# Attention and mixture of experts: one payload row for both experts, four payload and output buffers, neighbouring result rows

## What is computed

```python
h = layer_norm(x, ln1_w, ln1_b)
wei = softmax(where(causal, q @ k.T * C**-0.5, NEG_INF))   # 4 heads of 32, within a batch of 32 tokens
x = x + (wei @ v) @ Wo + bo
nx = layer_norm(x, ln2_w, ln2_b)
noisy = nx @ Wr + br + noise * softplus(nx @ Wn + bn)       # 8 experts
router_out = softmax(noisy with all but the top 2 at NEG_INF)
non_skip = sigmoid(nx @ Wsk + bsk) <= 0.5
expert_out = sum over e: router_out[e] * (relu(nx @ W1[e] + b1[e]) @ W2[e] + b2[e])
final = where(non_skip, x + expert_out, x)
```

## Time and profile before

| what | value |
|---|---|
| median of 3 executions | 811.3 us (807.3 to 813.56) |
| the profiled execution, its own time | 814.46 us |
| its span, first to last instruction | 812.5 us |
| busy share of the span | PE 71%, PEld 56%, DVE 71%, ACT 60%, POOL 51% |
| mean granted TensorE clock | 0.865 of 2.4 GHz |
| packets of the DMA queues | 164172, 127.32 MB |
| "instruction" packets in queues q8 and q14 | 27 and 17 |

### The profile page before, as it was taken

How to read it: one execution, slowest core, us unless ns; L and a number is a source line. 1 busy time by engine, 2 the same in 40 slices (tenths; PEclk the granted TensorE clock), 3 DMA queues, 4 the chain that set the end, 5 groups by cost and what they waited for, 6 DMA issues and landing times.

```text
span 812.5 us, 31537 instructions
## 1 busy us (share of the span) xinstructions
PE 579.6 (71%) x11012; PEld 455.5 (56%) x11012; DVE 576.5 (71%) x2270; ACT 486.9 (60%) x979; POOL 413.0 (51%) x478
## 2 busy tenths in 40 slices
PE   0466989989998998998865209999999999700000
PEld 0245767767776776777645207777777777500000
DVE  3366767887878788787664626777777777537887
ACT  2447666877877788687654208888888888400000
POOL 3000656677766777666655741666666666430000
PEclk9989989999999999999976559999999999855555
DMA  9764222332332332235443257777776777159997
GB/s 95 233 193 122 62 84 76 96 101 59 98 96 59 98 98 85 75 100 112 121 142 96 97 186 258 235 230 235 234 237 235 238 234 238 49 143 292 301 301 223
DMA packets 164172, 127.32 MB, mean 157 GB/s; under 512 B 38050, under 2 KB 142595, under 8 KB 164128
## 3 DMA queue, kind: packets, MB, share of 16 engines
q1 hardware_dynamic: 127264, 90.00, 37.8%
q10 hardware_dynamic: 24576, 20.98, 8.6%
q0 software_dynamic: 12288, 15.77, 6.1%
HBM read 73.86 MB, written 62.78 MB: 168 GB/s over the span
## 4 chain that ended last, share of the span: by engine, by line
PE 41%; DVE 22%; issue 14%; DMA 7%; ACT 5%; POOL 4%; DVEq 3%; ACTq 2%; SPq 1%; POOLq 0%
PE ps L547 6%; PE ps L504 6%; DMA out<-z 5%; DVE stats L830 4%; PE ps L569 4%; POOL expert_rows L1135 3%; PE ps L637 3%; PE ps L585 3%; PE ps L638 3%; PE ps L639 3%; PE ps L625 3%; PE ps L627 3%; PE ps L626 3%; DVE sc_m L873 2%; DVE smax L870 2%
## 5 line engine op out<-in xcount | busy, mean ns | idle before, releaser
L1135 POOL DMA_INDIRECT expert_rows<-pay,rows_of x256 | 254.2, 993 | 195.0 <-DVE rows_of L929 116.1
L1147 POOL DMA_INDIRECT expert_results<-z,words x128 | 135.1, 1055 | 106.9 <-DVE z L1028 75.6
L675 ACT ACTIVATE z<-xres,shift,rstd 128x128 f32 (+1 forms) x256 | 105.1, 483 | 34.4 <-DVE shift L864 34.4
L1042 DVE TENSOR_TENSOR hlo<-h,hhi 128x512 fp32r<-128x512 f32 x128 | 89.7, 701 | 45.7 <-ACT hhi L788 43.6
L786 ACT ACTIVATE h<-ps,w1x 128x512 f32<-128x512 f32 x128 | 88.3, 690 | 34.8 <-PE ps L627 31.3
L788 ACT ACTIVATE hhi<-ps,w1x 128x512 fp32r<-128x512 f32 x128 | 87.3, 682 | 0.0
L547 PEld LDWEIGHTS ps<-pT,v_sb 32*32 32x32 f32 x4096 | 48.4, 106 | 66.0 <-issue 64.6
L547 PE MATMUL ps<-pT,v_sb 32*32 32x32 f32 x4096 | 58.0, 204 | 35.7 <-DVE sc_m L873 25.2
L504 PE MATMUL ps<-ident,z 128*128 128x128 f32 x256 | 46.3, 310 | 25.8 <-ACT z L675 20.0
L637 PE MATMUL ps<-hhi,w2x 128*128 128x512 f32 x128 | 57.3, 447 | 4.2 <-issue 4.2
L527 PE MATMUL ps<-kT,qT 32*32 32x32 f32 x4096 | 55.8, 201 | 3.9
(11 more groups left out here) (147 smaller groups left out, 1321.5 us busy)
## 6 DMA issues: line engine op xcount, KB each, us to landing
w1x<-split_weights SPq DMA_DIRECT2D x33, 514.0 KB, 3.7
w2x<-split_weights SPq DMA_DIRECT2D x33, 512.5 KB
expert_results<-zeros SPq DMA_DIRECT2D x32, 512.0 KB
pay<-expert_rows SPq DMA_DIRECT2D x33, 264.0 KB, 3.6
xres<-in_r_x SPq DMA_DIRECT2D x32, 256.0 KB
split_weights<-w2x ACTq DMA_DIRECT2D x16, 512.0 KB
hhi<-expert_results SPq DMA_DIRECT2D x32, 256.0 KB, 3.7
hlo<-expert_results SPq DMA_DIRECT2D x32, 256.0 KB, 3.8
```

The lines of the kernel that those rows point to most:

```text
L675: m = nc.scalar.activation(z[:, j:j + 1], tile(xres, n, j), ACT.Identity, bias=shift[:, which, j:j + 1], scale=rstd[:, which, j:j + 1])
L1042: ev.tensor_tensor(hlo[:, c], h32[:, c % 2], hhi[:, c].bitcast(F32), ALU.subtract).then_inc(s_h_lo, 1)
L1135: g.indirect_dma_start(rows, bass.IndirectOffsetOnAxis(ap=rows_of[:, odd, k * J + j:k * J + j + 1], axis=0), pay[:, odd, k, j, :], None, b ...
L1147: g.indirect_dma_start(results, bass.IndirectOffsetOnAxis(ap=words[:, slot, j:j + 1], axis=0), yrow[slot][:, j, :], None, bounds_check=K * ...
```

## The change

- The payload is one row for both experts, with four buffers: `pay` is [P, 4, J, RW], as large as before. The second norm writes its rows into it in place, and TensorE transposes them from there. The copy L754 and its semaphore go.
- Word 128 is 2 x token. It is copied by ScalarE from a constant `words_all` just before the second norm. Words 129 and 130 are the token's two expert numbers (0 where the token skips), written by VectorE where it wrote `top_f` before. Pool's two operations a group go.
- `keep_words` makes the result's row from the row: word 128, plus 1 if word 129 is not this block's expert number (`exp_no`, one more operation for the table).
- `results` has a token's two results next to each other, so one DMA a group loads both, 1 KB a token.
- The combining accumulates in place in one of four `fin` buffers, and waits for the store of four groups before, ahead of its first half.
- `pipeline` has a body of four steps for all engines, since the payload's buffer number must be a constant in the code.

The diff, cut to its core:

```diff
-    results_t = results.rearrange("(k n p) c -> p k n c", k=K, p=P)
+    results_t = results.rearrange("(n p k) c -> p n k c", k=K, p=P)
...
-        pay = sb("pay", [P, 2, K, J, RW])
+        words_all = sb("words_all", [P, N // P])
+        pay = sb("pay", [P, 4, J, RW])
...
-        half = z1
-        fin = z2
+        fin = [z1[:, 0], z1[:, 1], z2[:, 0], z2[:, 1]]
+
+        xg = [pay[:, i] for i in range(4)]
...
         def pipeline(eng, step):
 
             for t in range(-2, 5):
-                step(t, t % 2)
-            with eng.Fori(5, NG - 4, 2) as t:
-                step(t, 1)
-                step(t + 1, 0)
+                step(t, t % 4)
+            with eng.Fori(5, NG - 6, 4) as t:
+                for d in range(4):
+                    step(t + d, (5 + d) % 4)
             for t in range(NG - 3, NG + 3):
-                step(t, t % 2)
+                step(t, t % 4)
...
-                for k in range(K):
-                    sp.dma_start(yin[slot][:, k], results_t[:, k, bass.ds(n * J, J), :]).then_inc(f_in[slot], 16)
+                sp.dma_start(yin[slot], results_t[:, bass.ds(n * J, J), :, :]).then_inc(f_in[slot], 16)
...
-                    transposes(ps[:, 6, :], z2[:, par], s_z2T_made)
+                    transposes(ps[:, 6, :], pay[:, (turn + 2) % 4, :, 0:C], s_z2T_made)
...
                     act.wait_ge(s_norm, (t + 3) * NORM)
-                    wait(act, s_z2T_made, n - 1)
-                    norm_rows(z2[:, par], 1, n).then_inc(s_z2, 1)
+                    slot = (turn + 2) % 4
+                    wait(act, sent[slot], quad(n, slot, SENT))
+                    nc.scalar.activation(pay[:, slot, :, C], words_all[:, bass.ds(n * J, J)], ACT.Copy)
+                    norm_rows(pay[:, slot, :, 0:C], 1, n).then_inc(s_z2, 1)
...
-                    wait(act, sent[par], pair(n, par, SENT))
-                    nc.scalar.activation(pay[:, par, :, :, 0:C], z2[:, par].unsqueeze(1).to_broadcast([P, K, J, C]),
-                                         ACT.Copy).then_inc(s_pay_made, 1)
...
-                    ev.scalar_tensor_tensor(top_f[:], top_i[:, :, 0:K].rearrange("p j k -> p k j"), 1.0,
-                                            keep[:, bass.ds(n * J, J)].unsqueeze(1).to_broadcast([P, K, J]),
+                    slot = (turn + 1) % 4
+                    wait(dve, sent[slot], quad(n, slot, SENT))
+                    experts_of = pay[:, slot, :, C + 1:C + 1 + K]
+                    ev.scalar_tensor_tensor(experts_of, top_i[:, :, 0:K], 1.0,
+                                            keep[:, bass.ds(n * J, J)].unsqueeze(2).to_broadcast([P, J, K]),
                                             ALU.add, ALU.mult).then_inc(s_route, 1)
...
+            ev.tensor_scalar(exp_no[:], exp_f[:], 1.0, None, ALU.add).then_inc(s_table, 1)
...
-                ev.tensor_copy(words[:, slot], xg[slot][:, :, C].bitcast(U32)).then_inc(s_words_kept, 1)
+                ev.scalar_tensor_tensor(words[:, slot], xg[slot][:, :, C + 1], exp_no[:, bass.ds(i, 1)],
+                                        xg[slot][:, :, C], ALU.not_equal, ALU.add).then_inc(s_words_kept, 1)
...
-                dve.wait_ge(f_in[slot], quad(n, slot, 16 * K) + 16 * K)
+                dve.wait_ge(f_in[slot], quad(n, slot, 16) + 16)
+                wait(dve, f_out[slot], quad(n, slot, 16))
...
                 dve.wait_ge(s_f_half, n + 1)
-                wait(dve, f_out[par], pair(n, par, 16))
...
-                    apart(pool, (sent[odd], pair(n, odd, SENT)),
-                                (s_token_next, n + 1))
-                    g.tensor_copy(pay_u[:, odd, :, :, C], token[:]).then_inc(s_word_made, 1)
-                    apart(pool, (s_word_made, n + 1))
-                    g.tensor_scalar(token[:], token[:], float(G), None, ALU.add).then_inc(s_token_next, 1)
+                    slot = (turn + 1) % 4
                     apart(pool, (s_route, n * ROUTE + ROUTE),
-                                (s_pay_made, n + 1))
+                                (s_z2, n + 1))
```

More of the change, by code:

```diff
@@ L147, in build @@
         rowhot = sb("rowhot", [P, K, J, E + 1])
-        rows_of = sb("rows_of", [P, 2, K * J], U32)
-        token = sb("token", [P, K, J])
-        pay = sb("pay", [P, 2, K, J, RW])
+        rows_of = sb("rows_of", [P, 4, K * J], U32)
+        words_all = sb("words_all", [P, N // P])
+        pay = sb("pay", [P, 4, J, RW])
         blocks_of = sb("blocks_of", [P, E])
@@ L166, in build @@
         exp_f = sb("exp_f", [P, MG + 1])
+        exp_no = sb("exp_no", [P, MG + 1])
         weights_at = sb("weights_at", [P, MG + 1], U32)
@@ L190, in build @@
         yin = [hhi[:, 0:K], hhi[:, K:2 * K], hlo[:, 0:K], hlo[:, K:2 * K]]
-        yin = [y.rearrange("p k (j c) -> p k j c", c=C).bitcast(F32) for y in yin]
-        half = z1
-        fin = z2
-        xg = [pay[:, i // 2, i % 2] for i in range(4)]
+        yin = [y.rearrange("p k (j c) -> p (k j) c", c=C).bitcast(F32) for y in yin]
+        yin = [y.rearrange("p (j k) c -> p j k c", k=K) for y in yin]
+        fin = [z1[:, 0], z1[:, 1], z2[:, 0], z2[:, 1]]
+        xg = [pay[:, i] for i in range(4)]
         yrow = [(z1, z2)[i // 2][:, i % 2] for i in range(4)]
@@ L311, in build @@
         s_f_out1 = sem("f_out1")
-        x_in, sent = [s_x_in0, s_x_in1], [s_sent0, s_sent1]
+        s_f_out2 = sem("f_out2")
+        s_f_out3 = sem("f_out3")
+        x_in, sent = [s_x_in0, s_x_in1], [s_sent0, s_sent1, s_sent2, s_sent3]
         w1_in, w2_in = [s_w1_in0, s_w1_in1, s_w1_in2, s_w1_in3], [s_w2_in0, s_w2_in1, s_w2_in2, s_w2_in3]
@@ L468, in _ @@
             for q in sent:
-                sp.wait_ge(q, SENT * NG // 2)
+                sp.wait_ge(q, SENT * NG // 4)
             def load_block(i, slot):
@@ L505, in transposes, with step @@
                 m.then_inc(ready, 1)
-            def step(t, par):
+            def step(t, turn):
+                par = turn % 2
                 odd = 1 - par
@@ L793, in _, with store @@
             blocks(nc.scalar, experts)
-            def store(n, par):
+            def store(n, slot):
                 act.wait_ge(s_f_made, n + 1)
[L798 to L802, removed]
+                act.dma_start(out_t[:, bass.ds(n * J, J), :], fin[slot]).then_inc(f_out[slot], 16)
+            with nc.scalar.Fori(0, NG - 3, 4) as n:
+                for d in range(4):
+                    store(n + d, d)
             for q in f_out:
-                act.wait_ge(q, 16 * NG // 2)
+                act.wait_ge(q, 16 * NG // 4)
         @block.vector
@@ L926, in step @@
                     dve.wait_ge(s_route, n * ROUTE + 13)
-                    wait(dve, sent[odd], pair(n, odd, SENT))
                     with nc.allow_low_precision(reason="whole numbers below 2**24 + 1"):
-                        ev.tensor_reduce(rows_of[:, odd].rearrange("p (k j) -> p k j", k=K), rowhot[:], AX.X,
+                        ev.tensor_reduce(rows_of[:, (turn + 1) % 4].rearrange("p (k j) -> p k j", k=K), rowhot[:], AX.X,
                                          ALU.add).then_inc(s_route, 1)
@@ L1119, in _, with step @@
             pool.wait_ge(s_blank_set, 1)
-            g.iota(blank_u[:, :, C:C + 1], [[0, J]], base=FAR, channel_multiplier=0).then_inc(s_blank_word, 1)
-            def step(t, par):
+            g.memset(blank[:, :, C:C + 1], float(FAR)).then_inc(s_blank_word, 1)
+            def step(t, turn):
+                par = turn % 2
                 odd = 1 - par
@@ L1135, in step @@
                             g.indirect_dma_start(rows, bass.IndirectOffsetOnAxis(
-                                ap=rows_of[:, odd, k * J + j:k * J + j + 1], axis=0),
-                                pay[:, odd, k, j, :], None, bounds_check=E * ER - 1,
-                                oob_is_err=False).then_inc(sent[odd], 16)
+                                ap=rows_of[:, slot, k * J + j:k * J + j + 1], axis=0),
+                                pay[:, slot, j, :], None, bounds_check=E * ER - 1,
+                                oob_is_err=False).then_inc(sent[slot], 16)
             pool.wait_ge(s_pay_zeroed, 1)
```

38 lines of the change are left out of this document (16 added, 22 removed).

## The result

The changed kernel takes 835.4 us (median of 4 executions, 831.26 to 836.74), the kernel before beside it 809.52 us (4 executions, 807.3 to 813.56). The ratio is 1.0305, with a 95% interval of 1.0246 to 1.0364: 3% slower. The forecast was 836, slower, 24.8 us over the 811.3 us known then. The profiled execution took 835.33 us (span 833.6), 20.9 us more than the one of before.

A forecast was written before the change was run, and what follows sets the result against it. TensorE and ScalarE bound the pipeline, TensorE the experts, DMA the combining. Fetches +23.5, jumps +7.5, ScalarE +1.2, Pool -4.3 and combining -3.1 sum to +24.8 us: 836 against the median of 811.3, range 804 to 856.

The forecast's parts named there:

- part 1: Pipeline loop: TensorE's four-step body grows from 5.5 to 11 instruction blocks; refetching costs +23.5 us, jumps back +7.5 us.
- share of three quarters: Pipeline loop: 23.5 us taken of the 31.4 us due if every pass fetched all 11 blocks.
- The jump's 7.5 us: Pipeline loop: five jumps back, each stopping TensorE 1.5 us for a fetch; bounds 0 and 13 us.
- rival C: Pipeline loop: everything is fetched and other engines miss at jumps; 848 or 856 us, within fetching's joint chance of 0.70.
- part 2: ScalarE in the pipeline: dropping the payload copy frees 0, the new copy of the words costs +1.2 us.
- part 3: Pool's tail behind the loop: 2.4 us from its dropped operations, 1.9 us from the payload copy, -4.3 us together.
- list of signs: What would show the forecast right; for Pool's tail, the last send 4 us sooner behind group 28's first.
- part 4: Expert stage: VectorE's word operation is of like size and TensorE sets the pace, so 0.
- part 5: Combining: DMA sets the pace; 1 KB loads and four output buffers save 0.1 us a group, -3.1 us.
- VectorE's floor of 2.48: Combining: VectorE's time per group with no store to wait for, 2.48 us; bounds the gain at -4.7 us.
- A: Pipeline loop: the four-step body stays in TensorE's instruction store, no fetches; -5.3 us, 806 us, chance 0.22.
- B: Pipeline loop: blocks are mostly kept and only the jump back costs; +1.3 us, 813 us, chance 0.08.

The follow-up runs named there:

- c4_all: Kernel before with a loop body of four steps on all engines, nothing else, on the second chip: 852.45 us, ratio 1.0465.
- c4_rest: Kernel before with a loop body of four steps on every engine but TensorE, on the second chip: 824.56 us, ratio 1.0147.
- c_pe2: Changed kernel with TensorE's looped steps in an inner loop of two, second chip: 813.97 us, ratio 1.0014 to the kernel before.
- b4_pe: Kernel before with a loop body of four steps on TensorE alone, on the first chip: 1042.88 us, ratio 1.0017.
- d_fin4: Kernel before with only the combining's four output buffers, loads as before, on the third chip: 1043.19 us, ratio 0.9904.
- b4_rest: Kernel before with a loop body of four steps on every engine but TensorE, on the first chip: 1047.58 us, ratio 1.0051.

## Why the prediction was right or wrong

**The loop's body (part 1), right in mechanism.** TensorE can't keep 11 blocks. The 60 blocks more are what fetching all of them in every pass gives: 5.5 for the two more steps in the code and 5 x 11 for the passes after the first. So the share of three quarters was wrong, and the whole body is fetched again. The Trainium skill ("Runtime: NRT & Kernel Launch", section "Instruction fetch mechanics") calls the instruction memory a FIFO that is refilled in blocks of 16 KiB. The 87 fetches agree with that.

The size was met by luck. The price was 31.0 in the sum (23.5 and 7.5), and TensorE's part measured 30.0 on the second chip (c4_all after c4_rest) and 22.1 in the changed kernel (after c_pe2, with the if in it), where the full share would have asked for 38.9. So a share too small met a price per pass too high. The price rested on one sample: the 5.7 us of the earlier trace rows were two stops (2.59 and 1.60 us) and 1.5 us of longer busy time at the lower clock. The same TensorE code ran through the same first-time steps in 45.4 us in c4_rest. What decides whether a fetch stops TensorE is not shown.

The jump's 7.5 us can't be told from the rest. TensorE's stop of 2.6 to 3.2 us behind a jump is there in b4_pe, but in the changed kernel it lies beside VectorE's.

**VectorE's store, missed.** The sum had it at 0, and only rival C named it, at 1.5 us a jump. It is 9.9 us in c4_rest, in stops of about 3 us; that is the price of the larger bodies of VectorE, ScalarE and Pool together, and the stops and q14's fetches point to VectorE. The hint stood in the trace of before: q14 fetched, too, and then not again in the loop.

**ScalarE (part 2).** The copy's going is worth nothing in the loop, as forecast. The +1.2 for the copy of the words wasn't seen: moving it away left the 22 steps where they were.

**Pool (part 3).** -4.3 was forecast and -2.5 measured from the add of t=29 to the last send. From group 28's first send to the last one it is 41.2 us after 45.2: 4.0 us sooner, as the list of signs had it, where the sum had only 2.4 for this. The part before that, forecast at -1.9, came out at +1.6. The start to t=7 came out 3.3 us shorter, unforeseen: TensorE's stop of 1.60 us is not in the first pass of the changed kernel. It is not in that of c4_rest either, whose TensorE code is the old one, so the new code isn't needed for that.

**Experts (part 4).** 235.1 after 235.4: nothing, as forecast.

**Combining (part 5), wrong by three times.** -3.1 was forecast and -9.2 measured. The step that failed is the reading of a DMA share of 1.00 as a limit. The share passes 1.00 when it is asked to (1.05 in the changed kernel's row above, at 333 GB/s, and 1.12 in d_fin4). The line that put a 1 KB packet at 51.5 ns was not far off, with 68.5% x 960 / 13522 = 48.6 ns in the changed kernel, but its pace bounded nothing. The second error was VectorE's floor of 2.48. It held a pause of 0.24 us before the second half, in the kernel before:

```profile
767.05 1.14 DVE L1067 SCALAR_TENSOR_TENSOR z<-hlo,gates,z 128x128 f32<-128x128 f32 x4 [0.24 <-DVE z L1061]
```

In the changed kernel a group takes 2.40 or less, with 0.15 us of waiting for its own first half (timeline of VectorE):

```profile
791.80 1.14 DVE L1066 SCALAR_TENSOR_TENSOR z<-hlo,gates,z 128x128 f32<-128x128 f32 x4 [0.15 <-DVE z L1061]
...
792.91 1.14 DVE L1061 SCALAR_TENSOR_TENSOR z<-hhi,gates,xres 128x128 f32<-128x128 f32 x4
...
794.20 1.14 DVE L1066 SCALAR_TENSOR_TENSOR z<-hhi,gates,z 128x128 f32<-128x128 f32 x4 [0.15 <-DVE z L1061]
...
795.26 1.13 DVE L1061 SCALAR_TENSOR_TENSOR z<-hhi,gates,xres 128x128 f32<-128x128 f32 x4
```

The sum held by luck as much as by its mechanism. The loop came out 4.0 us longer than forecast (36.2 for 32.2, TensorE's part smaller and VectorE's missing) and Pool's part 1.8, against 6.1 more gained in the combining and 3.3 at the start. These nearly cancel: by the profiles the change costs 20.9 us where 24.8 was forecast.

**The rivals.** A (kept) and B (only the jump costs) are excluded by 87 fetches. C was right that VectorE misses at the jump too; its 848 to 856 us were too many, since TensorE's fetches cost less than it took.

## What to carry to other kernels

A loop's body has a size in instructions, and doubling it for the sake of a constant buffer number on one engine doubles it for all. Before that, look at the instruction queues: a queue that fetches nothing in a loop is a gain that a larger body can lose. Code that runs for the first time shows that fetches can stop an engine, but not at what price: the same four steps took 45.4 and 53.5 us in two profiles. Giving each engine its own body, as short as its own constants allow, took the fetches away here; with both engines short it was measured only on a halting chip. A DMA share near 1.00 together with waits for a store's landing is first a question of buffers: four instead of two took some 9 us off the combining.

## What the runs showed of the hardware

- In a loop of 11 blocks of 16 KB every pass fetched all of them (87 against 27 fetches), and in one of 5.5 blocks none.
- The engines stop at different places: VectorE once a pass, at the jump, for about 3 us; TensorE at the jump as well (2.6 to 3.2 us in b4_pe) and amid lists, up to 2.7 us in the changed kernel.
- The clock is part of the price of a fetched body: of the 30.0 us between c4_rest and c4_all, 14.3 are longer busy time of the same matmuls, at a mean granted clock of 0.87 instead of 0.94.
- Two of the three chips of the experiments let TensorE through a list of 128 small matmuls only haltingly, one or two at a time after the first 27, with pauses of 0.3 to 2.0 us (b4_rest and d_fin4), and the kernel took 1042 to 1053 us instead of 810. On these a body of four steps cost about half a per cent at most (ratios 0.996 to 1.0051).
- Loads in pieces of 1 KB beside 512 B stores made the stores land in 5.1 instead of 3.7 us with two output buffers, and in 5.9 instead of 4.1 with four.
